# An fp4 rounding step with its tie factor folded into the ratio, and a last tile's down products on two halves of the partitions

## What is computed

```python
BLOCK = 16
_GRID = [0.0, 0.5, 1.0, 1.5, 2.0, 3.0, 4.0, 6.0]
_MID  = [0.25, 0.75, 1.25, 1.75, 2.5, 3.5, 5.0]

def fp4_quant_dequant(x):
    xb = x.reshape(shape[:-1] + (shape[-1] // BLOCK, BLOCK))
    scale = jnp.max(jnp.abs(xb), axis=-1, keepdims=True) / 6.0
    scale = jnp.maximum(scale, jnp.float32(1e-12))
    xn = xb / scale
    idx = jnp.searchsorted(_MID, jnp.abs(xn))
    q = _GRID[idx] * jnp.sign(xn) * scale
    return q.reshape(shape)

gate = fp4_linear(x, w_gate)          # both sides rounded; 256 -> 704
y = fp4_linear(x, w_up)
h = jax.nn.silu(gate) * y
return fp4_linear(h, w_down)          # 704 -> 256
...
h = h + _L0_ffn_ref(_layernorm(h, axis=-1), L0_ffn_w_gate, L0_ffn_w_up, L0_ffn_w_down)
```

## Time and profile before

| what | value |
| --- | --- |
| three runs, median (lowest to highest) | 288.36 us (287.0 to 288.85) |
| the profiled execution | 287.94 us |
| its span, first to last instruction | 286.1 us |
| mean granted TensorE clock, share of full speed | 0.988 |
| busy: PE / PE weight loads / DVE | 260.7 / 200.2 / 206.2 us |
| busy: ACT / POOL | 99.0 / 36.9 us |
| bytes read from HBM | 18.01 MB |

### The profile page before, as it was taken

How to read it: one execution, slowest core, us unless ns; L and a number is a source line. 1 busy time by engine, 2 the same in 40 slices (tenths; PEclk the granted TensorE clock), 3 DMA queues, 4 the chain that set the end, 5 groups by cost and what they waited for, 6 DMA issues and landing times.

```text
span 286.1 us, 10875 instructions
## 1 busy us (share of the span) xinstructions
PE 260.7 (91%) x4933; PEld 200.2 (70%) x4933; DVE 206.2 (72%) x411; ACT 99.0 (35%) x245; POOL 36.9 (13%) x35
## 2 busy tenths in 40 slices
PE   8999999999999999968798999997879899789865
PEld 8666678769899978858775766867766576655442
DVE  3659869999859976467688489564668664598992
ACT  1123301312010127557634432755554423361310
POOL 1991100152673000000000000000000000000000
PEclk9999999999999999999999999977999999999999
DMA  7999920000000000000004005200000000000001
GB/s 286 414 423 424 431 84 0 0 0 2 0 0 0 3 3 0 2 5 0 0 2 141 10 3 190 122 5 3 0 0 2 2 0 0 1 0 2 0 0 46
DMA packets 2727, 18.66 MB, mean 65 GB/s; under 512 B 464, under 2 KB 784, under 8 KB 1936
## 3 DMA queue, kind: packets, MB, share of 16 engines
q1 hardware_dynamic: 2704, 18.34, 16.1%
HBM read 18.01 MB, written 0.33 MB: 64 GB/s over the span
## 4 chain that ended last, share of the span: by engine, by line
PE 74%; DVE 17%; ACT 4%; issue 4%; POOL 0%; DVEq 0%; POOLq 0%
PE ps L1286 13%; PE ps L1606 8%; PE ps L1330 6%; PE ps L1344 5%; PE ps L1707 5%; PE ps L1797 5%; PE ps L1716 4%; PE ps L1589 3%; PE ps L1450 2%; DVE big L1134 2%; PE ps L1839 2%; DVE wt L1129 2%; PE ps L1276 2%; DVE big L1083 1%; PE ps L1318 1%
## 5 line engine op out<-in xcount | busy, mean ns | idle before, releaser
L1286 PE MATMUL ps<-big,cwb 128*128 128x384 f32 x112 | 37.9, 489 | 0.0
L1286 PEld LDWEIGHTS ps<-big,cwb 128*128 128x128 f32 x112 | 20.9, 190 | 13.0 <-DVE cwb L739 0.3
L1606 PE MATMUL ps<-xT,wl 128*128 128x320 f32 x88 | 24.5, 434 | 1.9 <-DVE xT L1175 1.9
L1716 PE MATMUL ps<-wt,big 32*32 32x32 f32 x1920 | 20.1, 195 | 4.4 <-issue 2.4
L1707 PE MATMUL ps<-wt,big 32*32 32x32 f32 x1600 | 17.9, 198 | 5.7 <-DVE big L1134 3.0
L1606 PEld LDWEIGHTS ps<-xT,wl 128*128 128x128 f32 x88 | 16.6, 190 | 8.9 <-ACT wguT L377 2.3
L295 POOL TENSOR_TENSOR xs<-xs,big 128x640 f32<-128x640 f32 x14 | 22.3, 1595 | 1.2
L1716 PEld LDWEIGHTS ps<-wt,big 32*32 32x32 f32 x1920 | 18.6, 106 | 5.2 <-issue 2.6
L1707 PEld LDWEIGHTS ps<-wt,big 32*32 32x32 f32 x1600 | 16.0, 109 | 8.1 <-DVE big L1134 4.0
L353 ACT COPY pecT<-ps 128x384 f32<-128x384 f32 x12 | 5.7, 478 | 39.8 <-PE ps L1286 39.8
L1129 DVE COPY_PREDICATED wt<-cst,ps 128x320 f32<-128x320 int32 x16 | 7.9, 496 | 13.1 <-PE ps L1716 13.1
(11 more groups left out here) (308 smaller groups left out, 507.7 us busy)
## 6 DMA issues: line engine op xcount, KB each, us to landing
big<-in_patches SPq DMA_DIRECT2D x6, 960.0 KB, 11.9
wl<-in_layers SPq DMA_DIRECT2D x2, 2176.0 KB, 19.8
wf<-in_ffn SPq DMA_DIRECT2D x1, 2112.0 KB, 18.1
wl<-in_layers SPq DMA_DIRECT2D x2, 1040.0 KB, 16.1
wt<-in_tok SPq DMA_DIRECT2D x1, 1536.0 KB, 25.0
wt<-in_tok SPq DMA_DIRECT2D x1, 768.0 KB, 8.5
cwb<-in_conv SPq DMA_DIRECT2D x1, 640.0 KB, 3.9
cst<-in_constants SPq DMA_DIRECT2D x1, 320.0 KB, 25.3
```

Source lines behind the costliest of these rows:

```text
L1286: last = mm(ps[:, i % 4, 0:GRP], cwc[:, k, c * P:(c + 1) * P], xg[:, g, k, :], start=(k == 0), stop=(k == KC - 1))
L1606: last = mm(ps[:, bank, 0:NT], w(c, j), x[:, c, :], start=(c == 0), stop=(c == CH - 1))
L1716: last = mm(ps[r, 6 + b, 32 * k:32 * k + 32], ttc[r, NB * b + k, :], yc[r, NB * b + k, :], start=True, stop=True)
```

## The change

Two edits, both in the code of the fp4 block.

First, the instruction L672, which multiplied the block reciprocals by `TIE_DOWN`, is gone; the ratio L679 is no longer a `tensor_tensor` but a `scalar_tensor_tensor`, which computes (value x TIE_DOWN) x reciprocal in one pass. This holds for all 11 quantizations.

Second, tile 2's down products are two sums of three: k = 3, 4, 5 go to PSUM partitions 64 to 127 of bank 6 and k = 0, 1, 2 to partitions 0 to 63, in the order 3, 0, 4, 1, 5, 2. The wait for the 96-row piece now stands before k = 5, again the fifth. `out_mm` is raised once after k = 5 and once after k = 2. DVE adds the upper sum to the residual first, waits for that add to be written, then adds the lower one.

```diff
@@ quant_scale, quant_step
                 step(v.reciprocal(ri, scl))
-                step(v.tensor_scalar(ri, ri, TIE_DOWN, None, ALU.mult))
...
-                step(v.tensor_tensor(r.rearrange("p (b n) -> p b n", n=16), src.rearrange("p (b n) -> p b n", n=16),
-                                     qs[0:p, 3 * k + 2, 0:nb].unsqueeze(2).broadcast_to([p, nb, 16]), ALU.mult))
+                step(v.scalar_tensor_tensor(r.rearrange("p (b n) -> p b n", n=16),
+                                            src.rearrange("p (b n) -> p b n", n=16), TIE_DOWN,
+                                            qs[0:p, 3 * k + 2, 0:nb].unsqueeze(2).broadcast_to([p, nb, 16]),
+                                            ALU.mult, ALU.mult))
@@ the last adds on DVE
-                v.tensor_tensor(h1[0:n, p, :], h1[0:n, p, :], ps[0:n, 6 + p % 2, 0:C], ALU.add
-                                ).then_inc(S["outs"], 1)
+                if p < 2:
+                    v.tensor_tensor(h1[:, p, :], h1[:, p, :], ps[:, 6 + p % 2, 0:C], ALU.add).then_inc(S["outs"], 1)
+                else:
+                    step(v.tensor_tensor(h1[0:64, p, :], h1[0:64, p, :], ps[64:P, 6, 0:C], ALU.add))
+                    dve.wait_ge(S["out_mm"], p + 2)
+                    v.tensor_tensor(h1[0:64, p, :], h1[0:64, p, :], ps[0:64, 6, 0:C], ALU.add).then_inc(S["outs"], 1)
@@ the down products on PE
-                order = range(FC) if p < 2 else (0, 3, 1, 4, 2, 5)
+                order = range(FC) if p < 2 else (3, 0, 4, 1, 5, 2)
...
-                    if p == 2 and k == 2:
+                    if p == 2 and k == 5:
                         pe.wait_ge(S["hqT"], 8)
...
-                        last = mm(ps[0:64, 6, 0:C], hq2[0:w, k % 3, 64 * (k // 3):64 * (k // 3) + 64], wdT[0:w, k, :],
-                                  start=(k == 0), stop=(k == FC - 1))
+                        a = k // 3
+                        last = mm(ps[64 * a:64 * a + 64, 6, 0:C], hq2[0:w, k % 3, 64 * a:64 * a + 64], wdT[0:w, k, :],
+                                  start=(k % 3 == 0), stop=(k % 3 == 2))
+                        if k == 5:
+                            last.then_inc(S["out_mm"], 1)
                 last.then_inc(S["out_mm"], 1)
```

## The result

Over 20 executions of each kernel on one chip the changed kernel took 286.86 us in the median, the kernel before 288.23. The ratio is 0.9945 with a 95% interval of 0.992 to 0.9969: 0.3 to 0.8% less, 1.6 us in the middle. The forecast was 1.35 us less, and no change by the bound of 1%. The ratio leaves out three executions of each kernel that were over 1.5% above its fastest, two of them, of the kernel before, at 520.87 and 626.09 us. The profiled execution took 286.37 us.

What follows compares the result with a forecast made beforehand. The chain was taken as 74% PE and 17% DVE, a relay of both at the end. Gains of 0.42 + 0.05 + 0.88 = 1.35 us off 288.36 gave 287.0 us, range 285.7 to 288.6.

Steps and rivals of the forecast that it cites:

- `hq` of tiles 0 and 1: Gated-value quantizations of tiles 0 and 1: both removed DVE steps are on the chain, gain 2 x 0.21 = 0.42 us.
- `hq` of tile 2: Tile 2's gated-value quantization: DVE and PE nearly level before, PE alone decides after the change, gain 0.
- `xq` and the weight pieces: Activation and weight quantizations: removed steps hidden by a table load, idle DVE or busy PE; gain 0 except 0.05 us.
- piece 2: Weight piece quantized a few us ahead of product L1007, for which PE's weight loads wait; gain 0.05 us, bounds 0 and 0.21.
- The fused multiply: The ratio as scalar_tensor_tensor instead of tensor_tensor: extra cost 0, bounds 0 and +0.06 us per instruction.
- The rival of a doubled streaming part: Fused ratio streams at half throughput, 0.75 us more per 704 columns, four on the path: 290.1 us; chance 0.05.
- Six pairs: Tile 2's down products on alternating partition halves run as six pairs side by side: 1.50 us instead of 2.82.
- The rival in which they don't pair: Tile 2's down products on separate halves still take 2.82 us, gain only 0.47: 287.9 us; chance 0.09.
- Two adds behind each other: After tile 2's down products: two DVE adds, none hidden, 0.87 us behind PE against 0.43; tail gain 0.88 us.
- The end follows: After the last add: SP is free for the last output DMA, so the kernel's end moves with the add.
- The margin for SP: At the end: the fourth output DMA's issue ends near 282.17, the last add at 282.50, so SP is free 0.3 us before.

Runs made afterwards that it cites:

- the last experiment: Changed kernel with the gated values' division by 6 also folded into the multiplies, in all three tiles; ratio 0.9903 (0.9862 to 0.9945) against the kernel before.
- part 1 alone: Kernel before with the tie factor folded into the ratio in all 11 quantizations, tile 2's down products as before; ratio 0.9966 (0.9925 to 1.0008).

## Why the prediction was right

The total came out as forecast, 1.6 us less by the ratio against 1.35. The interval, 0.9 to 2.3 us less, is too wide to tell a step of 0.2 us right from wrong, so the total holds in spite of the one that failed. The traces tell the steps:

- *`hq` of tiles 0 and 1, 0.42.* Measured 0.43, in every kernel with these two removals.
- *`hq` of tile 2, "PE alone decides. Gain 0".* This step failed. It is worth 0.21 to 0.22 us, shown by adding it alone (25.96 to 25.75) and by taking it alone out of the change (25.31 to 25.53). I had compared DVE's write at 279.59 with the end of PE's last record at 279.63 and called them level. But the transposes need not wait for that end. PE can follow 0.22 us after the start of the last record, at 279.26 + 0.22 = 279.48, so DVE decided before the change, with a start at 279.65. Afterwards the weights load at 278.91, 0.20 us before 276.25 + 2.86 = 279.11, as soon as DVE allows, and the transpose follows at 278.95, PE's earliest start. That PE decides now was right, but the gain up to there is not 0. Where DVE was faster still, in the last experiment, the gain stopped at 0.46 instead of 0.63 us, with the same 0.22 us between the two starts.
- *`xq` and the weight pieces, 0 but 0.05 for piece 2.* The zeros held: eight removals brought PE no nearer to the mark. The 0.05 was too much; DVE's gain became a wait of 0.28 us for PE.
- *The fused multiply, 0.* Held, 0.888 in the median at 704 columns with either form. The rival of a doubled streaming part, and with it the rule of the Trainium skill's "Vector Engine (DVE) Microarchitecture Reference" quoted ahead, section "Points that are easy to get wrong", falls for this form, f32 with an immediate factor: it would have shown about 1.65 us.
- *Six pairs, 1.50.* Measured 1.52 us from first start to last end. Two halves cost what one full record costs, as L1845 had shown at another width. The rival in which they don't pair is out. One reading on the way was wrong, without effect: two products of two records each are two pairs of records, so PE reached the fifth product 0.92 us after the first, not 0.44, and 1.78 before the change, not 0.9.
- *Two adds behind each other.* Both took what was forecast; the first started 0.03 us behind PE. I had said that the first hides nothing; it hides 0.04 us, the stagger between the two sums. The step as a whole gained 0.83 against the forecast 0.88, since the gap between the adds and their first waits came out a little longer.
- *The end follows.* It did, with -0.07. The margin for SP that I put at 0.3 us was 0.16, since tile 2's removal made the last add earlier than I had it, and the experiment without the upper add shows what happens when it is used up.

The mark's 0.09 us belongs to no part of the change: at 110 us, behind piece 2, the changed kernel's PE stood 0.04 us behind that of the kernel before, as it had at 20 us, and it came ahead by 0.28 only at 127, behind a pause of PE at 126 that was 0.37 us long in its chain and 0.70 before. In the eleven profiles that I have it lies between 252.54 and 256.50 us, with kernels that differ by nothing, or by DVE steps without effect, ahead of it. It goes for the most part with the clock and with stalls, see the last section. That is probably also why the intervals of the times are so wide, and it is why every verdict on a part above rests on marks within the last block.

## What to carry to other kernels

When a PE row shows no wait, look at the weight-load row beside it: if that one waited and the matmul starts with it, the engine it names sets the start, even where the matmul before it seems to end just then. PE's own limit is not that end but the start of the record before plus the usual spacing, here 0.22 us. Work out the worth of a removed small step only from what stands behind it, one place at a time: here 3 of 11 counted, for 0.65 us of a possible 2.3. Splitting a narrow sum over two halves of the partitions nearly halved PE's time for it here, from 2.82 to 1.52 us, and gave back an add and its completion wait; after that the next thing to ask is what the output queue is doing at that moment.

## What the runs showed of the hardware that I had not expected

- Matmuls on different halves of the output partitions don't keep strictly to the program's order. With three upper products ahead of three lower ones the lower ones ran beside the upper, beginning some 0.5 us after the first. By the starts in the trace six records of 128 rows had begun before the first one of 96 rows, at 282.43, and the upper sum has only four of 128 rows, so at least two lower ones ran ahead of its last product. Twelve records of 0.22 us spacing fitted into 2.00 us, where they would need 2.82 one behind another and at least 2.6 if the lower ones had to wait for the start of the last upper one. The Trainium skill's "TensorE: Matmul & The Clock Gate", section "Step-by-step: what each phase is for", says that only weight loads are pulled ahead and matmuls stay in program order. The trace does not fit that for matmuls on separate halves; one run shows it.
- Ahead of the last block the granted clock falls to 0.5 for stretches of a few us, and where it does so differs between executions of the same PE program. In windows of 5 us the kernel before and the changed one both had 0.66 at 185 and at 195 us, and marks at 254.59 and 254.50. The kernel with part 1 alone had one such stretch, at 125 us, and a mark at 253.30; the kernel with all removals but `hq` had lowered windows around 120, 185 and 195 us, and a mark at 255.92. Its PE stood 0.48 us behind that of the kernel before at 115 us, 1.55 at 120 and 1.30 at 127, so one such stretch cost about as much as either part of the change brings, and a good part of the 4 us between the marks goes with the clock. In the last block, behind the mark and while PE still had work, it fell in one of eleven profiles, where PE had paused 1.0 us for an ACT copy; it cost 1.7 us there, and in the other ten the same pause went by without it. The rows of two of them, the changed kernel and part 1 alone (stretch; length, PE busy and records, clock, DMA share, GB/s):

```profile
185.00:190.00 5.00, 5.00 (x80) 0.66 0.01 3
```
```profile
125.00:130.00 5.00, 3.79 (x304) 0.71 0.02 3
```

- The first pass of the level loop in the second layer has a stall on PE that no other engine explains. The chain gives it as "issue", 1.72 us in the kernel before, 1.83 in the changed one, and 0.46 in the first run with tile 2's removal alone, whose program ahead of that point is the same on PE:

```profile
192.84 1.72 issue
```
```profile
192.21 0.46 issue
```

  What sets it stays open; it was not tried. It is larger than either part of this change. In the seven profiles whose clock fell between 185 and 190 us and again between 195 and 200 it is 1.55 to 2.09 us, in the four others 0.36 to 0.64; which of the two brings the other is not shown.
